# Linear attention: VectorE's background tiles moved behind the step's additions to x, and the first output weight split ten steps before the first query

## The reference, cut to what matters

```
x = x + 0.5 * quantised_linear(layernorm(x))
x = x + linear_attention(layernorm(x))         # 16 query heads, 4 key/value heads, 128 wide
x = x + 0.5 * quantised_linear(layernorm(x))
x = x + 0.5 * routed_mlp(layernorm(x))         # scores all tokens, runs the best 128 of each batch
x = x + softmax_attention(layernorm(x))        # 16 heads
x = x + 0.5 * routed_mlp(layernorm(x))
```

```
q = phi(x Wq' + bq);  k = phi(x Wk' + bk);  v = x Wv' + bv
attn = (q (k' v)) / (q sum(k) + 1e-6);      x = x + attn Wo'
```

## Time and profile before

| | us |
|---|---|
| median of 3 runs | 3441.98 (3441.32 to 3443.99) |
| the profiled execution's own time | 3439.03 |
| its span in the profile | 3437.3 |
| busy: PE, DVE, ACT, POOL | 3336.6, 2671.8, 2042.7, 1059.2 |

### The profile page before, as it was taken

One profiled execution on the slowest core, in us unless ns is written; L12 is line 12 of the kernel. 1 busy time (PEld: TensorE's weight loads), 2 busy tenths in 40 slices (PEclk: granted clock), 3 DMA queues, 4 the chain that ended last, 5 costly groups with the idle time before them and its releaser, 6 DMA issues.

```text
span 3437.3 us, 53015 instructions
## 1 busy us (share of the span) xinstructions
PE 3336.6 (97%) x19523; PEld 2854.1 (83%) x19526; DVE 2671.8 (78%) x5155; ACT 2042.7 (59%) x3733; POOL 1059.2 (31%) x1293
## 2 busy tenths in 40 slices
PE   6899999999999999999999999999999999999997
PEld 4788888778888888888888888888888888888885
DVE  6899996778877778867888677886788767876776
ACT  4777777665556565555555656556555565556553
POOL 4887767522122122122121312212212121212112
PEclk9999999999999999999999999999999999999999
DMA  2222112200000000000000110000000010000000
GB/s 86 88 77 62 59 56 84 62 15 13 13 25 25 13 13 13 15 24 25 15 15 13 31 43 15 13 16 26 23 13 15 18 30 26 16 19 29 28 19 21
DMA packets 98528, 104.24 MB, mean 30 GB/s; under 512 B 10336, under 2 KB 88800, under 8 KB 98144
## 3 DMA queue, kind: packets, MB, share of 16 engines
q1 hardware_dynamic: 98272, 100.85, 9.7%
HBM read 87.18 MB, written 13.63 MB: 29 GB/s over the span
## 4 chain that ended last, share of the span: by engine, by line
PE 72%; DVE 5%; ACT 3%; issue 0%; POOL 0%; DVEq 0%; ACTq 0%; POOLq 0%
PE at_ps_job L2042 12%; PE at_ps_job L35 7%; PE at_ps_job L37 7%; PE at_ps_job L36 7%; PE at_ps_o L35 6%; PE at_ps_o L37 6%; PE at_ps_o L36 6%; PE at_ps_s L35 6%; PE at_ps_s L36 6%; PE at_ps_s L37 6%; DVE at_neg_max L1969 1%; ACT x_resident L1793 1%; DVE at_probT_lo L1836 1%; PE at_ps_job L656 1%; DVE li_wkv_lo L1867 0%; ACT at_probT_hi L1752 0%
## 5 line engine op out<-in xcount | busy, mean ns | idle before, releaser
L1752 ACT ACTIVATE at_probT_hi<-at_ps_job 128x512 fp32r<-128x512 f32 x1024 | 611.7, 598 | 889.1 <-PE at_ps_job L2042 886.8
L1836 DVE TENSOR_TENSOR at_probT_lo<-at_ps_job,at_probT_hi 128x512 fp32r<-128x512 f32 x1024 | 702.8, 686 | 273.0 <-ACT at_probT_hi L1752 262.5
L1793 ACT ACTIVATE x_resident<-at_ps_s,at_neg_max 128x1024 f32<-128x1024 f32 x512 | 570.9, 1115 | 149.5 <-DVE at_neg_max L1969 144.7
L1727 POOL TENSOR_TENSOR li_wkv_hi<-li_bkv,ch_cols 128x256 fp32r<-128x256 f32 x252 | 154.4, 613 | 1608.2 <-PE at_ps_job L37 1557.4
L1969 DVE TENSOR_REDUCE at_neg_max<-at_ps_s 128x1 f32<-128x1024 f32 x512 | 622.1, 1215 | 5.2
L2042 PE MATMUL at_ps_job<-ident,x_resident 128*128 128x128 f32 x4096 | 613.8, 272 | 4.7 <-DVE at_probT_lo L1836 3.0
L2042 PEld LDWEIGHTS at_ps_job<-ident,x_resident 128*128 128x128 f32 x4096 | 495.9, 140 | 97.6 <-issue 7.3
L35 PE MATMUL at_ps_o<-at_probT_hi,at_v_lo 128*128 128x512 f32 x1024 | 446.3, 436 | 7.5 <-DVE li_wkv_lo L1867 6.5
L35 PE MATMUL at_ps_s<-at_k_hi,at_q_lo 128*128 128x512 f32 x1024 | 445.1, 435 | 0.0
L37 PE MATMUL at_ps_o<-at_probT_lo,at_v_hi 128*128 128x512 f32 x1024 | 404.7, 395 | 0.0
L36 PE MATMUL at_ps_s<-at_k_hi,at_q_hi 128*128 128x512 f32 x1024 | 402.0, 393 | 0.0
(11 more groups left out here) (358 smaller groups left out, 7443.1 us busy)
## 6 DMA issues: line engine op xcount, KB each, us to landing
li_bkv<-attn_w SPq DMA_DIRECT2D x256, 128.0 KB, 2.3
li_bkv<-mlp_w SPq DMA_DIRECT2D x112, 128.0 KB, 2.3
li_wo_hi<-li_wo_kept SPq DMA_DIRECT2D x24, 256.0 KB, 2.6
li_wo_lo<-li_wo_kept SPq DMA_DIRECT2D x24, 256.0 KB, 3.0
li_wq_hi<-li_wq_kept SPq DMA_DIRECT2D x48, 128.0 KB, 2.1
li_wq_lo<-li_wq_kept SPq DMA_DIRECT2D x48, 128.0 KB, 2.3
x_resident<-x SPq DMA_DIRECT2D x4, 1024.0 KB, 12.7
out<-x_resident SPq DMA_DIRECT2D x4, 1024.0 KB, 4.9
```

The costliest lines, as they stand in the source:

```text
L1727: nc.gpsimd.tensor_tensor(hi, src, none, ALU.add).then_inc(s_wh[part], 1)
L1752: nc.scalar.activation(ph[:, i // TC, 4 * half:4 * half + 4, (i % TC) * P:(i % TC + 1) * P], c.turned_bank(2 * TB * u + 2 * i + half), ACT ...
L1793: nc.scalar.activation(prob[:, slot % 2, :], ps_s[slot % 2][:], ACT.Exp, bias=nmax[:, slot:slot + 1], accum_out=rsum[:, u % 2, slot:slot + ...
L1836: nc.vector.tensor_tensor(pl[at], c.turned_bank(2 * TB * u + 2 * i + half), ph[at].bitcast(F32), ALU.subtract).then_inc(s_pl, 1)
```

## The change

On DVE, the background's layer norm tiles (and FA's products with the router's weights and the bias on the logits) leave `dve_background` for a new function, `dve_background_tiles`. In the linear attention it is called at the end of the step, behind L1371 and L1378; in the softmax attention right behind `dve_background`, so that there only the order of the tiles and of L579/L581 in piece 6 changes. The waits inside are as before. The tiles of X, which have their own lines, stay.

On ACT and POOL, output weight 0 is split in step -10 instead of step -1. The other seven, and SP's order, stay.

More of the change, by code:

```diff
@@ L582, in dve_background @@
     if kind in ROUTED:
-        if 4 <= s < 10:
-            for j in LN_TILES[s - 4]:
-                layernorm_tile(nc, sh, c.tiles[:, j, :], c.x(b, j), j).then_inc(c.f_xn, 1)
-            for j in LN_TILES[s - 4]:
-                dve.wait_ge(c.f_xn, TB * n + j + 1)
-                nc.vector.tensor_tensor_reduce(out=c.junk[:, j * D:(j + 1) * D], in0=c.tiles[:, j, :], in1=c.wr[:], scale=1.0,
-                                               scalar=0.0, op0=ALU.mult, op1=ALU.add,
-                                               accum_out=c.logit[:, j:j + 1]).then_inc(c.f_dot, 1)
-        if s == 9:
-            dve.wait_ge(c.f_dot, TB * n + TB)
-            nc.vector.tensor_scalar(c.logit[:], c.logit[:], c.br[:, 0:1], None, ALU.add).then_inc(c.f_l, 1)
         if s == 13:
@@ L621, in dve_background @@
             nc.vector.tensor_tensor(c.ofl, c.o[:], c.ofh.bitcast(F32), ALU.subtract).then_inc(c.f_ol, 1)
+def dve_background_tiles(nc, dve, sh, c, t):
[4 more added lines that the diff above has]
+    if kind in QUANT and 4 <= s < 8:
+        for j in (2 * s - 8, 2 * s - 7):
+            layernorm_tile(nc, sh, c.tiles[:, j, :], c.x(b, j), j).then_inc(c.q_xn, 1)
+    if kind in ROUTED and 4 <= s < 10:
+        for j in LN_TILES[s - 4]:
+            layernorm_tile(nc, sh, c.tiles[:, j, :], c.x(b, j), j).then_inc(c.f_xn, 1)
+        for j in LN_TILES[s - 4]:
+            dve.wait_ge(c.f_xn, TB * n + j + 1)
+            nc.vector.tensor_tensor_reduce(out=c.junk[:, j * D:(j + 1) * D], in0=c.tiles[:, j, :], in1=c.wr[:], scale=1.0,
+                                           scalar=0.0, op0=ALU.mult, op1=ALU.add,
+                                           accum_out=c.logit[:, j:j + 1]).then_inc(c.f_dot, 1)
+        if s == 9:
+            dve.wait_ge(c.f_dot, TB * n + TB)
+            nc.vector.tensor_scalar(c.logit[:], c.logit[:], c.br[:, 0:1], None, ALU.add).then_inc(c.f_l, 1)
 def pe_background(nc, pe, sh, c, t):
@@ L1280, in _ @@
                                          scale=rnorm[:, m % 2, 3:4]).then_inc(s_y3, 1)
-                if made_time.get(t + 1, 2 * KVH) < 2 * KVH:
-                    i = made_time[t + 1]
+                if t in wo_step:
+                    i = wo_step[t]
                     act.wait_ge(s_wo, 16 * i + 16)
```

## The result

The median of 20 runs of the kernel after is 3446.19 us (3443.26 to 3449.04). Beside it the kernel before has 3440.84, also over 20 runs; one of those took 12043.92 us and is left out of the ratio, the others lie between 3436.69 and 3443.99. The ratio is 1.0016, with a 95% interval of 1.001 to 1.0022: 5.4 us more, slower by less than the 0.2% that I called "same". I had forecast +2.9 us, on a median of before that was 1.1 higher.

What follows compares the result with a forecast made beforehand. PE bounds most of the linear attention, but DVE (97 to 98% busy) bounds the four tile stretches. Weight 0 at -2.4 and +0.2 and the tiles at +5.1 give +2.9: 3444.9 us, range 3437 to 3451.

Steps and rivals of the forecast that it cites:

- Weight 0, -2.4 and +0.2: Start of the linear attention: the early split removes PE's 2.38 us wait, -2.4; POOL's later queue in the warm-up costs +0.2.
- The wait for POOL in the new place, 1.75 a pair: Tile steps: a tile pair starting 1.9 behind L1371 waits out POOL's L1175 and L1181, taking 1.75 us each time.
- Steps 67 to 72: Tiles and router products run through L1175, L1181 and L1185 in the new place: +3.5 us (2.0 to 4.6).
- Steps 49 to 52: Four pairs at 1.75 us, L1356 meeting L387, L579 freed, 0.54 less at the start: +1.0 us.
- Steps 29 to 32 and 5 to 8: Longer tile pairs, partly offset by other crossings with POOL falling away: +0.2 and +0.4 us.
- From the order alone I count no gain: Four tile stretches: DVE is full, and the L1371 behind the last tile step has everything in front as before; gain 0.
- The first rival: The order gains after all: each of the four stretches returns about one pair (1.7 us), giving 3433 us; chance 0.10.
- The second rival: Crossings of DVE with POOL cancel because POOL's order shifts too; only part 1, weight 0, counts: 3439.8 us; chance 0.22.
- The third rival: Router's logits become the bound: L1371 of step 73 and R come 6.5 later, +8.3 in all, 3450 us; chance 0.13.
- Those of being right: PE's wait at 88.23 gone, pairs at 1.7 to 1.8, DVE over 97%, step 67's to 73's L1371 about 5 longer than 30.1.
- sign of being wrong: Four tile stretches: pairs at 0.8 to 1.2, DVE gaps of a microsecond before L1363, or PE idle well under 19 us.
- The sum: Whole kernel: -2.4 + 0.2 + 5.1 = +2.9 us, the median going from 3441.98 to 3444.9.

Runs made afterwards that it cites:

- before_light: The kernel before, with POOL's three instructions behind phi cut to 16 columns around the tile steps; 3423.5 us, ratio 0.9953.
- weight_only: Against the kernel before: output weight 0 split in step -10, background tiles left at their old place; 3438.3 us, ratio 0.9996.
- the filler: The kernel after, with products of zeros added on PE in the five long waits of steps 8, 9, 10, 32 and 33; 3445.0 us, ratio 1.0016.
- quant_between: Kernel after, but quantised blocks' tiles between phi of the query and the additions to x, routed block's at their old place; 3433.51 us, ratio 0.9982.
- tiles_only: Against the kernel before: tiles at the end of the step, output weight 0 still split in step -1; 3446.83 us, ratio 1.0019.
- after_light: The kernel after, with POOL's three instructions behind phi cut to 16 columns around the tile steps; 3421.91 us, ratio 0.9951.
- routed_only: The kernel after, but only the routed layer's tiles (steps 67 to 72) at the end of the step, the quantised layers' where they were; 3440.99 us, ratio 1.0003.

## Why the prediction was right, and where it was not

**Weight 0, -2.4 and +0.2: right in place, and a little too good in size.** PE's wait is gone, and the chain behind it moved as said: less the shift of 1.61, phi of step 0 starts at 87.9 (predicted 87.6). The cost came where it was looked for: L1196 ends at 67.60 by the same reckoning (predicted 67.6), holds PE for 0.98 (predicted 0.8), and about 0.3 of that is left later in the warm-up. The net in every profile with the edit is -2.3 against the profile of before, where I said -2.2. But it is -1.7 against before_light, whose warm-up runs ahead of before's by 0.67 us from 65.73 on, and the medians give -1.9 (weight_only). So the early split costs 0.3 to 1.0, depending on the execution that it is set against, where I took 0.2.

**The wait for POOL in the new place, 1.75 a pair: right.** It is 1.84 in nearly every quiet step. Two experiments from opposite sides show the cause: the tiles 1.2 us earlier and POOL as it was (0.73), or the tiles as they were and POOL light (0.73). The Trainium skill, "SBUF — State Buffer", section "SBUF: two separate sides", gives this as a lock for a whole instruction, against VectorE operations in a 2-port mode or with two SBUF inputs. The runs agree also in whom it spares: in step 49 the last of the additions L1389, which read the accumulators, overlaps L1186 and takes 0.48 like the two before it, and the eviction L1311, which reads them too, starts inside L1196 and takes 0.68 as elsewhere.

**The size of it, cluster by cluster:**
- Steps 67 to 72, forecast +3.5 (2.0 to 4.6): +3.10, three times. Here the terms were right both ways. A step with two tiles and two products ran 1.85 and 1.42 and 0.41, ending 5.3 behind L1382 (said 5.6). The later pairs of L104 at 415.79 and 428.25 fell from 1.81 to 0.72, as said.
- Steps 49 to 52, forecast +1.0: +1.37 in two executions, +2.21 in the third. My own sum had a slip: the 1.54 is the tiles alone, and with L1356 (+0.8) and L579 (-1.1), less 0.54, it should have come to +0.7. The pairs take 0.1 us more than I took, and L1367 takes 1.12 where I said 0.9. The other 0.84 is one step, 52, and hangs on a hair: L1186 starts 0.06 behind the tile in both cases. With the filler the tile came first and L1186 took 1.50; in the kernel after, L1186 kept its 1.29 and both tiles waited (2.24).
- Steps 29 to 32 and 5 to 8, forecast +0.2 and +0.4: +1.60 and +1.87, and +1.02 and +2.77 in the execution with the tiles alone. These are the terms that were mis-sized. I had counted DVE's time and nothing else. DVE's busy time came out at -0.73 and -0.21, so that count was even too high. The step that I left out is what a late wait does to PE. By my own sentence the first L1371 of a cluster gains and the last has everything in front of it. So PE's waits for phi are not fewer (26.6 us against 24.8 from 92 to 669 us) but come late in the cluster (2.73 us at 137.25; 2.89 at 240.88 and 2.03 at 253.56), its clock is at the lower level behind them, and then it is PE that is late. With the clock kept up these clusters cost 0.86 and 0.22, against 0.4 and 0.2.

Was the clock new? No: the earlier trace rows has 0.92 for the same two stretches, and the mean of after is 0.93 and 0.94. What changed is where the slow matmuls lie. In the kernel before they lie amid the cluster, where PE waits for DVE anyway: steps 7 to 9 at a granted clock of 0.70 took 11.22, and 11.30 in quant_between at 1.00. In the kernel after they lie at its end, where PE has its backlog to work off. In the first cluster that holds for all three profiles with the quantised tiles in the new place and no filler (after, tiles_only, after_light), in the second for the first two of them. It is not fixed by the order alone: in routed_only, which has those tiles in the old place, the clock stayed at 1.00 behind a wait of 3.01 us at 124.74 and was low from 133.7 to 137.2, late in the cluster. In how many executions the new order pays for the clock is not known, and the total of the filler doesn't settle it.

**"From the order alone I count no gain": right.** With POOL light the two orders differ by +1.4 in the clusters, 1.1 of it steps 9 to 11 with the clock at 0.78 again (7.71 us; 6.59 in before_light). The rest is +1.00 in steps 48 to 55 and -0.95 in 66 to 74, so the order has effects of its own of up to 1 us, in both directions. The first rival (3433, by order) therefore fell, though a kernel of 3433.5 exists: it gets there by meeting POOL less often.

**The second rival, crossings that cancel: wrong here.** Had POOL's order shifted along with DVE's, a pair would have kept its old spread of 0.73 to 1.9. It became nearly constant, since POOL's L1186 is set off, through ACT's L1251, by the same L1382 as the tiles.

**The third rival, slower through the logits: little of it.** PE does wait behind the new place, in front of products that didn't wait there before (1.10 us for the eviction L1311 at 415.32, 1.35 at 427.79). But for the logits themselves R waits only 0.53 (at 443.79, for L630), and step 66 to 74 is +3.10, not +6.5.

**The signs named beforehand.** Those of being right came: from step 67's phi to step 73's it is 34.86 us, 4.77 more than the 30.1, where I said about 5. One sign of being wrong came too, a gap of a microsecond in front of L1363 (now L1374): 1.55 at 143.82. I would have read it as PE being held by the order and not by the amount of DVE's work. It was held by its clock there; with the filler that gap is gone.

**The sum.** Forecast -2.2 and +5.1, that is +2.9. By the medians of the parts alone it was -1.9 and +6.7, with +5.4 for both together: 2.5 more than forecast. In the profiled execution, which is slower than that median, the clusters cost 8.8, 3.7 above the forecast: 2.4 of it is gone in the filler's first two clusters, where the clock is kept up (2.1 in the two stretches shown), 0.8 is step 52, and the rest is crossings that were longer or shorter than I took them (+0.5 in steps 5 to 8, +0.4 in 49 to 52, -0.4 in 67 to 72).

Open: why the first stretch of the trace, up to 46.64 us before and 48.25 after, differs by 1.6 between executions, which of the two outcomes of step 52 is the usual one, and how often the clock is low at the end of the clusters. None was tried.

## What to carry to other kernels

Before you move a VectorE instruction that reads and writes SBUF, look up what GpSimd does at the new place, counted from the instruction that sets both off; if the same event releases both, expect the meeting every time. Where one engine is busy for 97% of a stretch, look for a gain in shorter instructions, so compare busy times with equal counts, not waits. And look at where the waits of the matmul engine fall: here slow matmuls amid a cluster cost nothing (11.22 us at a clock of 0.70, 11.30 at 1.00), while behind a wait just before the backlog they cost about 1 us.

## What the runs showed of the hardware

- A pair of tiles of 0.73 us takes 1.84 across GpSimd's L1186 and L1192 (1.29 and 0.79), and up to 2.75 across L387 and L1186 (1.32 and 1.34). One VectorE instruction slips in when a GpSimd instruction ends; the other waits out the next.
- Behind a wait of 2.73 us the granted clock was 0.78 over a stretch of 7.65 us. Thirty-six products of zeros in five waits kept it at 1.00 in both stretches where it mattered; the two stretches before them, steps 7 to 9 and 30 to 32, in which some 20 of them ran, took 13.53 against 13.50 and 13.63 against 13.53. A wait of this length is not always followed by the lower level: behind 3.03 us (before, 125.66) the clock was low, behind 3.01 (routed_only, 124.74) it was 1.00.
- Two executions with the same order in a step can differ by 0.84 us in it, when a VectorE and a GpSimd instruction come within 0.06 us of each other.
